# Spectral stage of a two-layer kernel: another order of the output chunks, the third tap place reloaded at the filter's end, mixing weights built in four portions

## The reference, cut to what matters

```python
for i, frac in enumerate((1, 2, 4, 8)):
    xi = x[:, :T // frac]
    si = _stu(xi, sigma, phi, M_u[i], M_phi_plus[i], M_phi_minus[i])   # causal filters, then mixing
    outs.append(pad(si))
return jnp.sum(stacked * weights, axis=-1)
```

## Time and profile before

| | before |
|---|---|
| median of 3 runs | 6822.46 us (6816.67 to 6832.06) |
| the profiled execution's own time | 6814.78 us |
| its span | 6813.0 us |
| granted TensorE clock, mean of the span | 0.949 |
| PE busy in the span | 5854.0 us (86%) |
| DVE busy | 4832.0 us (71%) |
| ACT busy | 3505.3 us (51%) |

### The profile page before, as it was taken

One profiled execution on the slowest core, in us unless ns is written; L12 is line 12 of the kernel. 1 busy time (PEld: TensorE's weight loads), 2 busy tenths in 40 slices (PEclk: granted clock), 3 DMA queues, 4 the chain that ended last, 5 costly groups with the idle time before them and its releaser, 6 DMA issues. The chain is left out here.

```text
span 6813.0 us, 130427 instructions
## 1 busy us (share of the span) xinstructions
PE 5854.0 (86%) x41691; PEld 5166.6 (76%) x41691; DVE 4832.0 (71%) x6902; ACT 3505.3 (51%) x7656; POOL 2748.9 (40%) x2143
## 2 busy tenths in 40 slices
PE   7789888988777898898987553899999989999998
PEld 5688788888656787888876342788888878888887
DVE  2799999999727999999997564456555555655555
ACT  2799999999636999999996221111111111111110
POOL 0588888888505888888886000000000000000000
PEclk8899999999888999999998886899999989999999
DMA  2122222222211222222222113766766666666665
GB/s 65 70 86 88 88 82 87 87 88 84 81 61 69 83 87 88 83 93 81 89 87 73 48 33 103 166 150 151 153 136 142 149 154 150 154 152 142 144 149 146
DMA packets 554833, 719.10 MB, mean 106 GB/s; under 512 B 38198, under 2 KB 458902, under 8 KB 520470
## 3 DMA queue, kind: packets, MB, share of 16 engines
q1 hardware_dynamic: 553814, 705.17, 38.3%
q10 hardware_dynamic: 720, 10.49, 0.4%
HBM read 677.22 MB, written 38.31 MB: 105 GB/s over the span
## 5 line engine op out<-in xcount | busy, mean ns | idle before, releaser
L656 POOL TENSOR_TENSOR read<-state,c_wide 128x1024 f32<-128x1024 f32 x1024 | 2434.8, 2378 | 460.9 <-DVE state L718 455.7
L718 DVE TENSOR_TENSOR_SCAN state<-decay,carry,p_drive 128x512 f32<-128x512 f32 x1792 | 2145.9, 1259 | 9.9 <-PE p_drive L503 8.4
L610 ACT ACTIVATE decay<-step,a_neg 128x512 f32<-128x512 f32 x2048 | 1416.2, 714 | 230.1 <-DVE state L718 229.8
L1573 PE MATMUL p_y<-window,x_high 128*128 128x256 f32 x7936 | 1502.7, 287 | 0.0
L1636 ACT COPY term_blocks<-p_s 128x256 f32<-128x256 f32 x832 | 309.9, 372 | 2191.2 <-PE p_s L1573 2191.2
L1573 PEld LDWEIGHTS p_y<-window,x_high 128*128 128x128 f32 x7936 | 1250.7, 192 | 0.0
L503 PE MATMUL p_drive<-diag_b,xu_tok 128*128 128x128 f32 x8192 | 1107.0, 286 | 119.2 <-DVE state L718 115.3
L503 PEld LDWEIGHTS p_drive<-diag_b,xu_tok 128*128 128x128 f32 x8192 | 1013.1, 197 | 212.0 <-DVE state L718 150.3
L1573 PE MATMUL p_y<-window,x_low 128*128 128x256 f32 x3968 | 1136.8, 286 | 0.0
L514 PE MATMUL p_y<-ident,read 128*128 128x128 f32 x8192 | 1077.3, 275 | 3.8 <-POOL read L656 3.8
L514 PEld LDWEIGHTS p_y<-ident,read 128*128 128x128 f32 x8192 | 941.4, 143 | 4.7 <-POOL read L656 4.7
(11 more groups left out here) (246 smaller groups left out, 5883.8 us busy)
## 6 DMA issues: line engine op xcount, KB each, us to landing
c_wide<-c_scratch SPq DMA_DIRECT2D x256, 1024.0 KB, 4.7
window<-taps_scratch SPq DMA_DIRECT2D x448, 257.0 KB, 6.2
window<-taps_scratch SPq DMA_DIRECT2D x768, 129.0 KB, 4.5
window<-taps_scratch SPq DMA_DIRECT2D x192, 513.0 KB, 7.0
window<-taps_scratch SPq DMA_DIRECT2D x64, 385.0 KB, 6.0
gate_scratch<-gate_out SPq DMA_DIRECT2D x16, 512.0 KB, 3.1
gate_in<-gate_scratch SPq DMA_DIRECT2D x16, 512.0 KB, 4.9
mix_weights<-in_M_plus SPq DMA_DIRECT2D x32, 256.0 KB, 7.0
```

The source lines that it names most:

```text
L610: act.activation(decay[:, n % 2, t, :], step[:, c.parity, t, :], ACT.Exp, scale=m.a_neg[:, DT2 * c.k + t, n:n + 1]).then_inc(s["decay"], 1)
L656: pool.tensor_tensor(read[:, n % 4, :, :], state[:, n % 4, :, :], wide, ALU.mult).then_inc(s["read_out"], 1)
L718: dve.tensor_tensor_scan(flip(state[:, n % 4, t, :], c), flip(decay[:, n % 2, t, :], c), flip(p_drive[:, n % 2, t, :], c), 0.0 if c.start ...
L1573: last = pe.matmul(out, x[:, source, blk, :], view[:, :, at:at + P][:, :, ::-1], start=first and x is m.x_high and z == 0, stop=True, skip ...
```

## The change: what it does

The order of the output groups becomes chunk 2 (slots 12 to 15), chunk 0 (16 to 19), chunk 3 (20 to 23), chunk 1 (24 to 27). The group that has no shared part is now group 8. Slot 20, no longer slot 16, waits for y, and its second product for w. SP loads the next filter's b after slot 23 (before: 19) and its c after slot 27 (before: 23), that is, just ahead of near of the next filter. `build` is cut into `sum_weights` (sum and first scaling) and `scale_weights` (three scaled additions), and runs after the joins of slots 3, 4, 5 and 6 for both kinds.

```diff
     ([(3, 256, 6)], 8), ([(3, 512, 4), (0, 256, 8)], 10),
+    ([], 0), ([(0, 256, 0)], 2),
     ([(3, 768, 2), (1, 256, 10)], 12), ([(3, 1024, 0), (1, 512, 8), (0, 256, 12)], 14),
     ([(1, 256, 2)], 4), ([(1, 512, 0), (0, 256, 4)], 6),
-    ([], 0), ([(0, 256, 0)], 2),
 ]
-CHUNKS = (2, 3, 1, 0)
-NO_SHARED = 12
+CHUNKS = (2, 0, 3, 1)
+NO_SHARED = 8
@@ sync, load of the following filter
                 load("a", following)
-                sp.wait_ge(s["made"], START + n * SLOTS + 20)
+                sp.wait_ge(s["made"], START + n * SLOTS + 24)
                 load("b", following)
-                sp.wait_ge(s["made"], START + n * SLOTS + 24)
+                sp.wait_ge(s["made"], START + n * SLOTS + SLOTS)
                 load("c", following)
@@ tensor, slot
-                for at, name in ((0, "a"), (4, "b"), (8, "c"), (12, "near"), (12, "x"), (16, "y")):
+                for at, name in ((0, "a"), (4, "b"), (8, "c"), (12, "near"), (12, "x"), (20, "y")):
...
-                    if i == 16 and v == 1:
+                    if i == 20 and v == 1:
                         pe.wait_ge(s["in_w"], ...)
@@ vector
-            def build(n, k, kind):
+            def sum_weights(n, k, kind):
                 if kind == 0:
                     dve.wait_ge(s["m_in"], START + n * 32 + 32)
+                else:
+                    dve.wait_ge(s["mix_now"], START + n * 2 + 1)
                 (sum, m_read for kind 1, first scaling, as before)
+            def scale_weights(n, k, kind):
                 (the three scaled additions, as before)
@@ vector, body
                     if i == 2:
                         if not first:
                             add(n + -1, 3)
-                        build(n, k, 0)
+                    if i in (3, 5):
+                        sum_weights(n, k, (i - 3) // 2)
+                    if i in (4, 6):
+                        scale_weights(n, k, (i - 4) // 2)
...
-                    if i == 11:
-                        build(n, k, 1)
```

More of the change, by code:

```diff
@@ L1117 @@
     ([(3, 256, 6)], 8), ([(3, 512, 4), (0, 256, 8)], 10),
[1 row of a table added]
     ([(3, 768, 2), (1, 256, 10)], 12), ([(3, 1024, 0), (1, 512, 8), (0, 256, 12)], 14),
     ([(1, 256, 2)], 4), ([(1, 512, 0), (0, 256, 4)], 6),
[1 row of a table removed]
 ]
 SLOTS = 2 * len(GROUPS)
-CHUNKS = (2, 3, 1, 0)
-NO_SHARED = 12
+CHUNKS = (2, 0, 3, 1)
+NO_SHARED = 8
+TERM_OF = {6: (0, 0, False), 7: (3, 3, False), 10: (1, 1, False), 11: (2, 2, True), 12: (5, 0, False), 13: (5, 5, True)}
 RUNS = {
@@ L1690, in with_term @@
                     dve.tensor_tensor(out[:, :, P:NEAR], t[:, :, P:NEAR], both, ALU.subtract).then_inc(s["merged"], 1)
-                dve.wait_ge(s["merged"], START + n * 12 + (i - 11))
+                dve.wait_ge(s["merged"], START + n * 12 + (i - 11 if i < 16 else i - 15))
                 dve.wait_ge(s["made"], START + n * SLOTS + (i + 1))
@@ L1702, in join @@
                 to = filtered[:, (g - 6) // 2 % 2, source, :, g % 2 * NEAR:g % 2 * NEAR + NEAR]
-                if g < 12:
-                    term, at, minus = ((0, 0, False), (3, 3, False), (1, 1, False), (2, 2, True), (5, 0, False),
-                                       (5, 5, True))[g - 6]
+                if g in TERM_OF:
+                    term, at, minus = TERM_OF[g]
                     with_term(n, i, to, source, term, at, minus)
```

## The result

The changed kernel takes 6961.57 us (median of 4 runs, 6958.99 to 6969.49), beside 6819.57 for the kernel before in the same comparison (6806.20 to 6832.06). The ratio is 1.0211, 95% interval 1.0189 to 1.0232: slower by 142 us, where 130 (6952 us) were forecast. The profiled execution took 6958.99 us with a span of 6957.3.

What follows compares the result with a forecast made beforehand. TensorE was taken to bound the loop, waiting for tap windows and VectorE. Late x made +4.5 us in 30 filters (+135), filter 16 gave -5: +130 on 6814.8, 6945, plus 7.7 to the median, 6952 us; range 6785 to 7040.

Steps and rivals of the forecast that it cites:

- The c release: At the filter's start c, near and x queue back to back, so x lands and slot 12 starts at 25.3 us.
- The source of the number: Filter 0's first loads: c, near and x take 20.9 us back to back, at 204 GB/s with engines 92% busy.
- The estimate of 12.5 us for 4.47 MB: Skill's DMA rule for c, near and x: x there at about 15 us, slot 12 never waits; rival's chance 0.12.
- The wait at slot 16: The wait for w goes, all 51.0 us and its clock, as w gets 10 us more time.
- The length of the wait: TensorE idles about 3.4 us at slot 12, from 21.9 to 25.3 us.
- The clock: Matmuls behind the slot 12 wait run at a lower clock, losing 2.0 us a filter, bounds 0 and 3.4.
- The weights: Both builds before slot 8's join let VectorE start slot 12 at 21.9, costing nothing beside the wait for x.
- the rival that would have made the kernel faster: VectorE bounds slot 12 if x lands before 21.9: 76.1 us a filter, 6790 us in all; chance 0.12.
- c at slot 8: c lands at 12.75 us, slot 8 is ready at about 12.4: a 0.35 us wait, hidden by what comes.
- The sum: 25.3 + 54.2 + 2.0 = 81.5 us a filter against 77.0, +4.5 for 30 filters; filter 16 gains 5; in all +130.

Runs made afterwards that it cites:

- The kept c: The changed kernel with c loaded once for filter 0 and its reload at each filter's end left out: 6779.12 us, ratio 0.9908 to the kernel before.
- the moved releases: The kernel before, old order and weights, with only the loads of b and c released later (after slots 23 and 27): 7013.96 us, ratio 1.0247.
- the fastest kernel: The changed kernel with chunk order 0, 2, 3, 1 and both weight builds after the joins of slots 13 and 15: 6758.16 us, ratio 0.9865.

## Why the prediction was right

- **The c release**, the step that decided, held in mechanism and size. Slot 12 was to start at 25.3; it started at 25.8 in the filter shown and at 25.9 on average, 25.5 us in that filter after the first issue of c for the 25 forecast. The kept c and the moved releases show that this and nothing else makes the loss.
- **The source of the number** was filter 0 of the kernel before: the one place where c, near and x had run back to back. The estimate of 12.5 us for 4.47 MB (the Trainium skill, "DMA: Bandwidth & Descriptors", "Specifications" and "Anatomy of one DMA") did not hold for these loads: 217 GB/s moved with the engines 93% busy. That section gives its fit for DMAs that GpSimd issues, and these are SyncE's; what makes them slower than the estimate was not tried.
- **The wait at slot 16** went in every filter, as forecast.
- **The length of the wait** at slot 12 was put too short, 3.4 us for 5.15 in that filter. The start of slot 12 was right; the forecast counted the wait from where VectorE would let slot 12 go, 21.9. TensorE waits from the end of slot 11, which was at 20.65; VectorE would have let slot 12 go at 21.2. Of the 1.75 us that were missing, 0.5 are x landing later, 0.7 VectorE being earlier and 0.5 slot 11 ending before that. The last two change nothing in the filter's length.
- **The clock** was taken as 2.0 us a filter; it is 2.1 in the filter shown and 56.2 - 54.2 = 2.0 on average.
- **The weights** were costed at nothing beside the wait for x. With them back in their old places the ratio did not move beyond its interval. Their price alone, a later join of slot 8, was put at 2.5 us and was 21.0 - 19.2 = 1.8. The forecast took the length of the first kind's build for the second as well; the last section has both. As the bound at slot 12, the rival that would have made the kernel faster, they appear when c is kept: 75.9 us a filter for the rival's 76.1, slot 12 at 21.4 for its 21.9.
- **c at slot 8** was to wait 0.35 us. Of the 51 waits for windows 29 stand at slot 12 (143.6 us); the other 22 are at slot 8, 1.2 us each, and with the two named in the result c lands late in 24 of 31 filters. As forecast, slot 12 waits for x behind this in nearly all of them; in the fastest kernel it is the main wait that is left.
- **The sum** was +4.5 us a filter against +5.1 measured (82.06 - 76.98), and the 0.6 are x landing at 25.9 and not at 25.3. It was to hold 30 times and held 28 times, +142 in all. Filters 15 and 31, the last of each batch, lost only 1.7 and 2.9 us, and filter 16 gained 6.8 where 5 was forecast. Together this makes the +140 of the loop behind filter 0, so the near hit of +130 has a little luck in it: the error of each filter and those of the three special ones partly cancel.

## What to carry to other kernels

When a load is moved, write down everything that is queued behind it on its engine until the next wait, and read the time of that sequence from a place where the trace already has it back to back, such as the first turn of a loop. A place that is held longer gives its next load back later, so the consumer of what is *behind* that load pays. If the late window can't come sooner, let the order of the work want it later; and take an engine's side jobs out of the stretch where its joins hold the others.

## What the runs showed of the hardware that I had not expected

- The two builds have the same five operations and not the same length. In the kernel before the first kind took 5139.87 to 5142.41 = 2.5 us in one piece, and the second, behind slot 11 of the same filter, 5155.60 to 5157.81 = 2.2:

```profile
5155.60 0.68 DVE L1657 TENSOR_TENSOR mix_weights<-mix_weights 128x512 f32<-128x512 f32 x1
5156.44 0.29 DVE L1663 TENSOR_SCALAR mix_weights<-mix_weights,frac_filter 128x128 f32<-128x128 f32 x1 [0.16 <-DVE mix_weights L1657]
5156.77 1.13 DVE L1667 SCALAR_TENSOR_TENSOR mix_weights<-mix_weights,frac_filter 128x128 f32<-128x128 f32 x3
5157.81 0.42 DVE L1689 TENSOR_TENSOR term_blocks<-term_blocks 128x256 f32<-128x256 f32 x1
```

- Cut in portions with other work between, each was a little cheaper: 1.02 + 1.27 = 2.29 us for the first kind and 1.05 + 1.03 = 2.08 for the second, in filter 10 of the changed kernel. The two together are 4.37 us where one of 2.54 stood, which is the 1.8 us by which the join of slot 8 came later. The rows show short waits of VectorE for its own last result, 0.16 us each, at some steps of a build and not at others. Why they are at these steps, and that they are the whole difference, was not tried.
